# A decoder layer's attention loop: the values product cut in three pieces, the packed tile's transposes in two, divisions two maxima later

## The reference, cut to what matters

```python
q = (x @ Wq).reshape(B, T, 16, 32); k = ...; v = ...      # 16 heads of 32
scores = jnp.einsum('bthd,bshd->bhts', q, k)
scores = scores * jnp.tril(ones)                           # masked scores are 0, not -inf
attn = jax.nn.softmax(scores / T ** 0.5, axis=-1)
out = jnp.einsum('bhts,bshd->bthd', attn, v).reshape(B, T, 512)
x = x + out @ Wo
```

## Time and profile before

| | us |
|---|---|
| median of 3 runs | 1484.2 (1483.01 to 1485.87) |
| the profiled execution's own time | 1483.99 |
| its span in the profile | 1482.3 |
| the four attention passes, from the first transpose to the last | 70.3 to 127.1, 202.3 to 259.8, 334.2 to 391.0, 470.8 to 529.8 |
| PE busy over the span | 1427.4 (96%) |
| ACT busy over the span | 720.3 (49%) |
| DVE busy over the span | 985.7 (66%) |

### The profile page before, as it was taken

The page is one execution under the profiler, slowest core; times in us unless marked ns, Lnnn a source line. Parts: engine busy times, 40 slices in busy tenths (PEclk is TensorE's granted clock), DMA queues, the critical chain, the costliest instruction groups (busy, mean ns, idle before and its releaser), DMA issues.

```text
span 1482.3 us, 26838 instructions
## 1 busy us (share of the span) xinstructions
PE 1427.4 (96%) x8896; PEld 720.6 (49%) x8896; DVE 985.7 (66%) x2113; ACT 720.3 (49%) x1672; POOL 379.9 (26%) x691
## 2 busy tenths in 40 slices
PE   6989999998998899999999999999999999999999
PEld 4465456556644654344444444444444444444444
DVE  7785687678567767887566666655665765665533
ACT  5795279239616945254353353353343442533432
POOL 0053224304373436522211112112112212212100
PEclk9999999999999999999999999999999999999999
DMA  7553522352455521001000001001001001000011
GB/s 248 136 164 124 156 85 85 112 158 66 147 154 150 185 79 45 17 16 33 23 14 29 17 17 33 17 17 35 17 17 33 17 16 33 16 17 1 1 57 57
DMA packets 76877, 98.01 MB, mean 66 GB/s; under 512 B 8000, under 2 KB 60736, under 8 KB 76224
## 3 DMA queue, kind: packets, MB, share of 16 engines
q1 hardware_dynamic: 76736, 96.23, 21.1%
HBM read 68.94 MB, written 27.26 MB: 65 GB/s over the span
## 4 chain that ended last, share of the span: by engine, by line
PE 79%; DVE 7%; ACT 7%; issue 6%; POOL 1%; DMA 0%; ACTq 0%; DVEq 0%; POOLq 0%; SPq 0%
PE bank L863 23%; PE bank L865 23%; PE bank L864 23%; ACT prob L1244 3%; PE bank L948 2%; PE bank L927 2%; PE bank L1003 1%; PE bank L876 1%; ACT prob_t L1260 1%; PE bank L916 1%; PE bank L957 1%; PE bank L998 1%; PE bank L988 1%; DVE G L1705 1%; DVE c L1730 1%
## 5 line engine op out<-in xcount | busy, mean ns | idle before, releaser
L863 PE MATMUL bank<-xs,G 128*128 128x512 f16 x896 | 339.8, 379 | 2.8 <-ACT c L1332 1.2
L864 PE MATMUL bank<-xs,G 128*128 128x512 f16 x896 | 339.6, 379 | 0.0
L865 PE MATMUL bank<-xs,G 128*128 128x512 f16 x896 | 339.6, 379 | 0.0
L1332 ACT COPY c<-bank 128x512 f32<-128x512 f32 x192 | 111.2, 579 | 220.3 <-PE bank L865 215.5
L1716 DVE TENSOR_TENSOR c<-bank,c 128x512 f32<-128x512 f32 x128 | 88.1, 689 | 192.9 <-PE bank L865 192.9
L863 PE MATMUL bank<-Wd,hid 128*128 128x512 f16 x512 | 194.1, 379 | 2.8 <-DVE X L1770 2.8
L864 PE MATMUL bank<-Wd,hid 128*128 128x512 f16 x512 | 194.0, 379 | 0.0
L865 PE MATMUL bank<-Wd,hid 128*128 128x512 f16 x512 | 194.0, 379 | 0.0
L735 POOL TENSOR_TENSOR c<-c,m 128x512 f32<-128x512 f32 x64 | 82.2, 1284 | 390.0 <-ACT c L1332 390.0
L1770 DVE SCALAR_TENSOR_TENSOR X<-bank,col,X 128x512 f32<-128x512 f32 x128 | 95.4, 750 | 101.4 <-PE bank L865 101.3
L1586 DVE CUSTOM_DVE_ANT_0 bank<-bank,mask,col 128x128 f32<-128x128 f32 (+3 forms) x256 | 139.5, 550 | 28.4 <-issue 14.1
(11 more groups left out here) (192 smaller groups left out, 2402.3 us busy)
## 6 DMA issues: line engine op xcount, KB each, us to landing
stack<-qk_dram SPq DMA_DIRECT2D x128, 128.0 KB, 3.3
sc_in<-scale_t SPq DMA_DIRECT2D x30, 384.0 KB
qk_dram<-qk SPq DMA_DIRECT2D x32, 256.0 KB, 2.8
packed_t<-pk_t SPq DMA_DIRECT2D x32, 192.0 KB, 2.0
pk_in<-packed_t SPq DMA_DIRECT2D x30, 192.0 KB
X<-in_x_dram SPq DMA_DIRECT2D x4, 1024.0 KB, 6.0
pk_in<-L_ffn_gate_W_packed_dram SPq DMA_DIRECT2D x16, 256.0 KB, 2.7
pk_in<-n_L_ffn_up_W_packed_dram SPq DMA_DIRECT2D x16, 256.0 KB, 3.1
```

Source lines behind the costliest of these rows:

```text
L863: pe.matmul(o, lhs(0), rhs(0), start=first, stop=False, skip_group_check=onto)
L864: pe.matmul(o, lhs(0), rhs(1), start=False, stop=False, skip_group_check=onto)
L865: return pe.matmul(o, lhs(1), rhs(0), start=False, stop=stop, skip_group_check=onto)
L1332: nc.scalar.copy(dst[:], bank[BANK_Y if which == M5 else x][:]).then_inc(c_copied, 1)
```

## The change

On PE, `values` of unit u - 1 no longer stands whole at step (u, 3). One block stays there (piece 0); piece 1, one block, goes behind the transposes of (u + 1, 0), and piece 2, whatever is left (none, one or two blocks), behind those of (u + 1, 1). Units 13, 14 and 15 keep theirs whole. The waits of `values` stand before piece 0, the one for `v_zero` and the signal `av_done` at the last piece. The two halves of `repack` move apart: the first stays at step (4r + 4, 1), the second goes to (4r + 4, 2). With that the slots are counted anew: the second half gets the slot behind turn (4r + 4, 2).

On DVE, the division of u - 3 comes at j = 2 and not at j = 0, and the copy of the second packed half at (4r + 5, 3) and not at (4r + 5, 0). On ACT, `out_head` moves from j = 0 to j = 2 (tile 2); on POOL, `out_tail` moves from behind (tile 2, head 3) to behind (tile 3, head 0).

```diff
@@ slots
-            return h + 2 * (max(0, h - 2) // 16) + max(0, h // 4 - 1)
+            return h + max(0, h - 2) // 16 + max(0, h - 3) // 16 + max(0, h // 4 - 1)
 
         def pack_slot(r, half):
-            return (turn_slot(16 * r + 17) + 1 if r < HG - 1 else recip_slot(UNITS - 2) + 1) + half
+            return turn_slot(16 * r + 17 + half) + 1 if r < HG - 1 else recip_slot(UNITS - 2) + 1 + half
...
-        AT_RECIP, AT_DIVIDE = 9, 12
+        AT_RECIP, AT_DIVIDE = 9, 14
         AT_SUMS, AT_TURNED, AT_RECIPROCALS = 1, 3, 2
-        AT_OUT = 0
+        AT_OUT = 2
@@ POOL
-                        if j == 3 and i == 2 and r > 0:
+                        if j == 0 and i == 3 and r > 0:
                             out_tail(n, r - 1)
@@ PE, values
-            def values(n, u):
+            def values(n, u, piece=None):
...
+                total = blocks + (i < TT - 1)
+                if piece is None:
+                    ks = range(total)
+                else:
+                    ks = {2: (range(1), range(1, 2), range(0)), 3: (range(1), range(1, 2), range(2, 3)),
+                          4: (range(1), range(1, 2), range(2, 4))}[total][piece]
...
-                mm.then_inc(av_done, 1)
+                if ks.stop == total:
+                    mm.then_inc(av_done, 1)
@@ PE, loop
                         if j == 3 and u > 0:
                             recips(n, u - 1)
-                            if u < UNITS - 1:
+                            if u < UNITS - 2:
+                                values(n, u - 1, 0)
+                            elif u == UNITS - 2:
                                 values(n, u - 1)
-                        if j == 1 and u % TT == 0 and u > 0:
-                            repack(n, u // TT - 1)
+                        if j < 2 and 1 < u < UNITS - 1:
+                            values(n, u - 2, j + 1)
+                        if j in (1, 2) and u % TT == 0 and u > 0:
+                            repack(n, u // TT - 1, j - 1)
@@ DVE, loop
-                        if h >= 0 and h % 4 == 0:
+                        if 0 <= h < 4 * (UNITS - 3) and h % 4 == 0:
                             divide(n, h // 4)
-                        if j == 0 and u % TT == 1 and u > TT:
+                        if j == 3 and u % TT == 1 and u > TT:
                             repacked(n, u // TT - 1)
```

More of the change, by code:

```diff
@@ L928, in turn @@
                 mm.then_inc(t_full, 1)
-            def values(n, u):
+            def values(n, u, piece=None):
                 hg, i = u // TT, u % TT
[L933 to L938, removed]
-                blocks = wide[i] // P
+                blocks = wide[i] // P
+                total = blocks + (i < TT - 1)
[4 more added lines that the diff above has]
+                          4: (range(1), range(1, 2), range(2, 4))}[total][piece]
+                if len(ks) == 0:
+                    return
+                if ks.start == 0:
+                    pe.wait_ge(pt_act, n * 3 * UNITS + 3 * u + 3)
+                    pe.wait_ge(pt_dve, n * UNITS + u + 1)
+                    if u == 0:
+                        pe.wait_ge(v_out, n * TT + TT)
+                    if u >= 1:
+                        pe.wait_ge(o_done, n * UNITS + u)
                 at = P * (u % 2)
-                if i < TT - 1:
+                if i < TT - 1 and ks.stop == total:
                     pe.wait_ge(v_zero_done, beyond_units(n, u))
-                for k in range(blocks + (i < TT - 1)):
+                for k in ks:
                     for j in range(4):
@@ L1010, in context_out, with repack @@
                     mm.then_inc(att_full, 1)
-            def repack(n, r):
+            def repack(n, r, half):
                 nb = n * (NB // B) + r
                 pe.wait_ge(pk_conv, 6 * nb + 6)
[L1015 to L1024, removed]
+                pe.wait_ge(*turn_read(n, pack_slot(r, half) - 3))
+                bk = turn_bank(pack_slot(r, half))[:].bitcast(F16)
+                tiles = [[(0, 0), (1, 0)], [(0, 1), (1, 1)], [(2, 0), (3, 0)]] if half == 0 else \
+                        [[(2, 1), (3, 1)], [(4, 0), (4, 1)], [(5, 0), (5, 1)]]
+                for q in range(3):
+                    for e, (a, w) in enumerate(tiles[q]):
+                        mm = pe.transpose(bk[:, 256 * q + P * e:256 * q + P * e + P], pk_16[:, a, P * w:P * w + P], ident16[:])
+                mm.then_inc(pk_full, 1)
             def product(m, x, which, pair, slot, nb):
@@ L1200, in body @@
                             recips(n, u - 1)
-                            if u < UNITS - 1:
+                            if u < UNITS - 2:
+                                values(n, u - 1, 0)
+                            elif u == UNITS - 2:
                                 values(n, u - 1)
-                        if j == 1 and u % TT == 0 and u > 0:
-                            repack(n, u // TT - 1)
-                repack(n, HG - 1)
+                        if j < 2 and 1 < u < UNITS - 1:
+                            values(n, u - 2, j + 1)
+                        if j in (1, 2) and u % TT == 0 and u > 0:
+                            repack(n, u // TT - 1, j - 1)
+                repack(n, HG - 1, 0)
+                repack(n, HG - 1, 1)
                 recips(n, UNITS - 1)
```

## The result

| | before | after |
|---|---|---|
| median (four runs each) | 1483.61 us (1482.22 to 1485.87) | 1526.04 us (1525.02 to 1526.39) |
| ratio, 95% interval | | 1.0287 [1.0275, 1.0300] |
| span of the profiled execution | 1482.3 | 1523.2 |
| ACT's waits for a transpose or for `values` before the copies of heads 0 to 2 | 9.7 in 28 waits | 48.1 in 50 waits |

The changed kernel is 42.4 us slower; 1519 was forecast, with a range of 1500 to 1534. In the changed code `turned` on ACT is L1274, `exp` L1258, `values` L957, `recips` L967, `divide` L1638, and DVE's `row_max` L1600.

What follows compares the result with a forecast made beforehand. ACT was taken to bound an attention pass. 2.88 us for each four units, three groups and 0.17 at the end make 8.8 us a pass, 35.2 in four: 1483.99 + 35.2 = 1519.2, said as 1519; range 1500 to 1534.

Steps and rivals of the forecast that it cites:

- What bounds a pass: In an attention pass ACT is full, 54.12 of 56 us; PE time costs only where ACT waits; relief 6.7 us.
- rival A: ACT's six waits in a pass go and nothing replaces them: 1477.5 us; any gain over 0.2%, 6%.
- The new wait: ACT's head 0 copy waits for `av_done`, now sent with the last piece: 1.03, 0.66, 1.06 us at units 11, 12, 13.
- tile 3: Unit 11: ACT's copy of head 0 comes at 375.45, wanted at 374.42; cost 1.03 us.
- tile 0, less the old 0.18: Unit 12: ACT waits 0.84 us in place of 0.18 before the copy of head 0; cost 0.66 us.
- tile 1, less the old 0.38: Unit 13: ACT waits 1.44 us in place of 0.38 before the copy of head 0; cost 1.06 us.
- tile 2: Unit 14: `av_done` arrives within 0.1 us of when it is wanted, covered by exps; cost nothing, bound 0 to 0.3 us.
- copy of the reciprocals and the rest of the period: At unit 13, `recips` of unit 11 wait for ACT's copy of (12, 2); ACT's reciprocal copy is late by 0.13 us.
- the end of the last piece: A block is complete 0.40 us after it starts, each further one 0.22 more; ACT starts 0.04 us after the end.
- Where the division holds PE: Division two maxima later: `values` piece 0 waits for it at unit 11, some 0.6 us of PE, included in that unit's cost.
- Rival C: Late exps hold `e_zero`, sums, division and piece 0; unit 14 waits 0.5 us and more: 1536 and above, 5%.
- B: After unit 11's wait, units 12 and 13 find pieces done: 18 us, 1502; with what lies between (1487.2 to 1508), 18%.

Runs made afterwards that it cites:

- pieces alone: `values` in three pieces on the kernel before; divisions, halves of `o_sum` and packed tile as before: 1512.49 us, ratio 1.0189.
- the divisions alone: Divisions two maxima later and both halves of `o_sum` moved with them, on the kernel before; `values` whole, packed tile as before: 1501.45 us, ratio 1.0117.
- the version with two pieces: Kernel before with `values` in two pieces, three buffers for all heads of the transposed tile, divisions one maximum later: 1485.59 us, ratio 1.0014.
- the one with three pieces: Kernel before with `values` in three pieces, three transposed-tile buffers, divisions one maximum later, packed halves ahead of piece 2: 1475.46 us, ratio 0.9946.
- three buffers alone: Third buffer for all four heads of the transposed tile, nothing else, on the kernel before: 1482.01 us, ratio 0.9989.

## Why the prediction was right, and where its sum was off

**What bounds a pass, and rival A.** Right. PE time did not matter and ACT's waits did; the relief of at most 6.7 us was real, if smaller in three of the four passes, and shown only once the new wait was taken away (1475.5 against Rival A's 1477.5).

**The new wait.** Right, and shown: with PE's order untouched and one more buffer, 33 of 42 us go. The reading of the trace of before on which it stood, that the transposes of (u, 1) start too late for anything behind them to be complete when ACT wants head 0, held at tiles 3, 0 and 1. At tile 2 it left something out (below).

**The terms for each group of four units.**

| place | predicted | change in full | pieces alone |
|---|---|---|---|
| tile 3 | 1.03 | 1.06 | 1.12 to 1.20 |
| tile 0, less the old 0.18 | 0.66 | 0.76 | 0.76 |
| tile 1, less the old 0.38 | 1.06 | 1.20 | 0.86 |
| tile 2 | 0 (bound 0.3) | 0.41 (6 of 12) | none |
| copy of the reciprocals and the rest of the period | 0.13 | 0.3 | 0.2 |
| group's period, over 15.1 | 2.88 | 3.75 | 2.95 |

The last line is the distance of two copies of tile 0. The row before it is what is left of that distance; a reciprocal copy that starts late shows no wait of its own, so that it is the late reciprocals was argued, not shown.

Two of the prices behind these terms held nearly to the digit. In the earlier trace rows a change of tile width was read as 0.12 us in and 0.11 out; the changed kernel has 0.23 us from a transpose to a piece in the rows

```profile
388.69 0.30 PE L927 MATMUL bank<-ident,prob 128*128 128x128 f32 x1
388.92 0.43 PE L957 MATMUL bank<-prob_t,V 128*32 128x128 f32 x8
389.28 0.28 PE L916 MATMUL bank<-stack 128*128 128x256 f16 x1
```

and 0.36 from a piece to the scores (0.33 predicted).

**The term that was mis-sized: the end of the last piece.** The prediction had ACT start 0.44 us after a last piece of one block starts (0.40 for the block and the 0.04 read behind transposes), and 0.22 later with two. The changed kernel has 0.55 (399.14 to 399.69, below) and 0.77 (394.66 to 395.43): ACT starts 0.12 us after the end that the profile gives for the block, not 0.04. That is 0.11 us at each of the 36 copies of head 0 at tiles 3, 0 and 1, 4.0 us in all. At tile 1 it is the whole difference between the 1.95 us that the chain from the transposes to ACT's copy takes (393.48 to 395.43) and the 1.85 worked out.

**Where the division holds PE.** The prediction said of the later division that `values` piece 0 waits for it "at unit 11 for some 0.6 us of PE, included above", and gave it nothing else. That was wrong. At tile 3 piece 0 waits for ACT's copy of head 2,

```profile
383.50 0.43 PE L957 MATMUL bank<-prob_t,V 128*32 128x128 f32 x8 [0.50 <-ACT prob_t L1274]
```

and at tile 1 it follows `recips` after 0.24 us as before (392.62, 392.86). In the whole third pass PE waits for a division three times, 2.3 us together, all at tile 2. With `values` whole it waits 5.6 us in eight (the run with the divisions alone), and there the late divisions cost 17.6 us. Divisions and split packed tile together add 13.7 us to the cut product (42.4 less 28.7).

That the pieces alone have a group of 2.95 us over the old one, next to the forecast sum of 2.88, is partly luck. The forecast held a late packed copy of DVE at tile 1, and the pieces alone don't have it (0.86 there in place of 1.20: in the changed kernel the transposes at 393.48 wait for that copy); three ends of pieces, 0.11 each, make up for it.

**Tile 2, which I costed at nothing.** The timeline there shows the division's part:

```profile
396.47 0.16 DVE L1618 SCALAR_TENSOR_TENSOR den_all<-e_zero,den 128x4 f32<-128x4 f32 x1 [1.09 <-ACT e_zero L1267]
396.55 0.63 DVE L1573 TENSOR_SCALAR xn<-X,mv,rs 128x512 f32<-128x512 f32 x1
397.11 0.61 DVE L1600 CUSTOM_DVE_ANT_0 bank<-bank,mask,col 128x384 f32<-128x384 f32 x1
...
397.74 0.25 DVE L1638 SCALAR_TENSOR_TENSOR o_sum<-bank,r_den 128x128 f32<-128x128 f32 x1
...
398.14 0.42 PE L957 MATMUL bank<-prob_t,V 128*32 128x128 f32 x8 [0.90 <-DVE o_sum L1638]
...
398.72 0.49 PE L927 MATMUL bank<-ident,prob 128*128 128x128 f32 x3
...
399.14 0.43 PE L957 MATMUL bank<-ident,v_zero 128*32 128x128 f32 x8
...
399.69 0.48 ACT L1274 COPY prob_t<-bank 128x384 f32<-128x384 f32 x1 [0.41 <-PE bank L957]
```

The copy of head 0 that came 1.58 us late holds `e_zero`, and DVE's sums wait 1.09 us for it. The division, which before stood ahead of these sums, now stands behind them. Piece 0 waits 0.90 us for the division, and piece 1, with the signal, comes behind it all. With the divisions early the wait is not there at all. But the late division doesn't make it by itself either: between the sums and the next maximum stands `xn` (L1573), a part of the next batch element's normalisation, which DVE has at units 4, 6, 8 and 10 of every pass but the last. In the fourth pass, at unit 10, the sums wait just as long and the wait of ACT's copy is gone:

```profile
543.68 0.16 DVE L1618 SCALAR_TENSOR_TENSOR den_all<-e_zero,den 128x4 f32<-128x4 f32 x1 [1.09 <-ACT e_zero L1267]
...
544.95 0.43 PE L957 MATMUL bank<-prob_t,V 128*32 128x128 f32 x8 [0.50 <-DVE o_sum L1638]
...
546.50 0.48 ACT L1274 COPY prob_t<-bank 128x384 f32<-128x384 f32 x1
```

Piece 0 waits 0.50 us there and 0.90 with `xn`; the 0.40 between them is ACT's wait of 0.41. Unit 14, which has no `xn` part, doesn't wait in any pass. No run takes `xn` away alone, but the two kinds of unit 10 stand in one execution. So the chain is the one that Rival C named, at 0.41 us where the rival wanted 0.5, and at units 6 and 10 and not at unit 14.

**Where the 7.2 us are that the sum fell short.** Before its copies of heads 0 to 2 ACT idles 48.1 us in place of 9.7. That is 38.4 more, where the sum had 33.7 (35.2 less 12 x 0.13 for the reciprocals). The ends of the pieces add 4.0 and tile 2 adds 6 x 0.41 = 2.5. Against that, 1.4 us of the old 9.7 belong to one wait of 1.59 us in the fourth pass, where its like elsewhere is 0.19, and the end of a pass costs 0.1 in place of 0.17. The other 4.0 us of the 42.4 stand before no copy of heads 0 to 2; the sum had 1.6 for them, and what the remaining 2.4 are wasn't settled.

**Rivals.** B did not happen: tiles 0 and 1 wait in full after tile 3. The reason given, that the next unit's chain starts with an exp behind the late copy, agrees with those waits; no run tested it apart. **Signs.** The group's period was forecast at 18.0 and is 18.9; ACT's waits before the copies of head 0 were forecast at about 9 us in a pass and are 11.6. None was to stand in units 6, 10 and 14; units 6 and 10 have one in three passes, unit 14, named as what would make the forecast wrong, has none. The waits of 0.1 us before the copies of the reciprocals don't show. ACT's share fell to 82%, forecast 84%. The clock and the MLP did not change.

**What stays open.** Why three blocks and not one before the packed transposes cost the version with two pieces 10 us over the one with three pieces was read from a wait of DVE (1.3 us), not tested by itself. And of the five versions that were to come out at the kernel before or under it, none met its forecast: four were slower, each time because the next wait was one that I had costed as covered, and the last was faster (1475.46 where 1477 to 1483 was expected).

## What to carry to other kernels

When a product is cut in pieces to let something else through, its "done" signal moves to the last piece: before cutting it, look up who waits for that signal, when it is wanted in the old trace, and what the last piece now stands behind; where the buffers are two, a third one comes first. An instruction that is moved later costs nothing up to its slack and then stops what is queued behind its waiter: size it at each kind of unit and in each pass, by what now stands between it and what it waits for; here 0.6 us of work for the next batch element decided whether anybody felt it. Take out waits one at a time, and expect the next edit that "cost nothing" to show its price then.

## What the runs showed of the hardware that I had not expected

In this kernel one maximum of delay of a division cost 0.0% and two cost 1.2% (with `out_tail` moved too): nearer to a step than to a slope. The releaser that a row names can be the wrong one where an instruction waits for two things: in the earlier trace rows the transposes at 374.63 are put down to exp, whose last row for that head ended at 373.71; DVE's copy ended at 374.48, 0.15 us ahead, and the pattern repeats after a packed copy that ended 0.14 us ahead. And in the fourth pass of the kernel before PE stands 1.01 us in the middle of a `values`, at 484.38, with no releaser; that pass took 59.0 us where the other three took 57.6, and 56.5 in the fastest version, where it is as long as its fellows. Such stalls stand in other runs too: 1.56 us at 485.02 with three buffers alone, 2.30 at 484.16 with the divisions one maximum later, each in the middle of a `values`, and the 2.53 us in the MLP of the change with `values` whole, behind which the granted clock was 0.66 from 1038 to 1043 us and 1.00 after. What they are wasn't settled.
